# A two-layer decoder kernel: 28 passes in one turn of the loop in place of seven turns of four

## The chip, the cores and the metric

The kernel runs on one core of one Trainium2 chip. The metric is the device time of one execution in microseconds (us). Times of a kernel are medians over several executions; a profile is one further execution, recorded by the hardware profiler. The engines are TensorE (PE; its weight loads are listed as PEld), VectorE (DVE), ScalarE (ACT), GpSimd (POOL) and SyncE (SP), which here issues all the DMAs.

## What is computed

For each of 32 batches (256 tokens x 256 features) two decoder layers are computed, in float32:

```
x = x + latent_attention(layernorm(x))        # 16 heads, softmax over tokens
x = x + cross_attention(layernorm(x), ctx)    # 16 heads of 64, softmax over heads per token
x = x + routed_ffn(layernorm(x))              # the best 128 of 256 tokens go through the FFN
x = x + topk_attention(layernorm(x))          # the best 25 scores per row are kept
x = x + cross_attention(layernorm(x), ctx)    # masked by a length per batch
x = x + ternary_linear(layernorm(x))
```

## The kernel before, in words

The work on a batch is cut into four stages, each with a letter: **m** (latent attention), **h** (cross attention with the routed FFN), **t** (top-k attention), **c** (masked cross attention and the last linear layer). The stages form a pipeline over batches. In one *pass* m works on batch i+3, h on i+2, t on i+1 and c on i. A stage hands its rows to the next one through single buffers (`xin` from m to h, `xa` from h to t, `x4` from t to c), so a stage's next pass begins when the stage ahead of it has finished this one.

Each stage is written as a generator for each engine, and every `yield` in it ends a step. The order in which an engine's steps of the four stages are interleaved is a string of letters, one string for each engine (`ORDER["pe"]`, ...); `woven` takes one step of the named stage for each letter. Each engine executes its instructions in that order, and semaphore waits do the rest. The strings of `ORDER` hold four passes (`LAPS = 4`). The last letters of a string may name a stage whose four passes are already over; such a letter issues nothing.

`passes` emits one such stretch: a block with all five engines, then a second block in which SP clears all the semaphores. At the end of each block the engines meet in a barrier (lines 1295 and 1340 in the profile). The stretches are `start`, `first`, the loop, and `last`. The loop (line 1350) executes its one stretch of four passes seven times, jumps back after each time, and is called here seven *turns*. Since the semaphores are cleared, every count of a wait starts again in each turn. `past` emits a wait for the pass before, and emits none in a turn's first pass, where the barrier stands for it.

The instructions that stand around a turn's end and beginning, by line: L795 (PE) is the last matmul of stage h, and L919 (DVE) adds its result to `xa`, the last instruction of the turn on DVE. L712 (PE) projects `ctxA` for the next batch in stage h, and the first 16 of these matmul records are a turn's first on PE. L402, L406 and L419 (DVE) and L411 and L414 (POOL) are the layer norms; L429 (PE) transposes the normed rows; L442 and L450 (PE) are projections; L1020 (DVE) copies the values of stage t and is the first DVE instruction that needs a projection. SP's queue loads `ctxB` and the length (L1303), `xin` (L1310) and `ctxA` (L1313), and stores the result (L1317), in this order in each pass.

Of the kernel before, what the change touches and what calls it, by code (L numbers as in the profile page):

```python
# [133 lines left out]
        t5 m t h t h m t3 h t2 h c2 t h c t7 h2 t4 m t3 h2 t2 c t h t6 c t2 h t m t h c h t3 h t3 c t9 h t3 h m h t3 m t2 h t c t c t h t2 h  # L134
        c t4 h2 t2 m t2 c t3 h2 m t9 h c2 t2 h t h t h t6 c t2 h t7 h t2 m t h t3 m h t h t2 c3 t2 h t4 h2 t h t5 m t3 h2 t3 h t5 c h t2"""),
}
LAPS = 4

FILL = {"t": ["00020100", "02010111", "00020101", "02010011"],
        "h": ["20111000100", "00211000000", "00121000100", "01111100000"],  # L140
# [24 lines left out]
def program(nc, x_in, ctx_in, lens_in, w_in, out):  # L165
    es = ExitStack()
    with es:
# [196 lines left out]
        lap = {"n": 0}  # L364
        first, last = {}, {}
# [27 lines left out]
        def fill(letter, place, to):  # L393

            table = {"loop": FILL, "first": FILL_FIRST, "last": FILL_LAST}.get(lap["of"], {})
            if letter in table:
                for _ in range(int(table[letter][lap["n"] - first[letter]][place])):
                    nc.tensor.matmul(to, w["xwq"][:, 0, 0:P], w["xwq"][:, 1, 0:P], start=True, stop=True)

        def ln_dve(dve, k, x, ln):  # L400
# [279 lines left out]
        def tensor_h(pe):  # L680
# [34 lines left out]
            for s in range(QUADS + 3):  # L715
# [21 lines left out]
                if s >= 3:  # L737
                    q = s - 3
                    yield
                    pe.wait_ge(*at(g["hm_pt"], q + 1))  # L740
                    fill("h", q, bankH[1][:, D:D + P])
                    for uh in range(2):
                        for jo in range(2):
                            i = jo * 2 + uh
                            last = nc.tensor.matmul(bankH[1][jo * XD:(jo + 1) * XD, uh * P:(uh + 1) * P],
                                                    xv[:, 4 * q + i, :], xpt[q % 2][:, i, :], start=True, stop=True)
                    last.then_inc(g["hm_o"], 1)
# [11 lines left out]
            for d in range(ND):  # L759
                last = nc.tensor.matmul(bankH[0][:, 0:S], w["wrt"][:, d, :], lnH["xT"][:, d, :], start=(d == 0), stop=(d == ND - 1))  # L760
            last.then_inc(g["md_sps"], 1)
            fill("h", 8, bankH[1][:, 0:P])
            yield
            pe.wait_ge(*at(g["md_e"], 6))
            fill("h", 9, bankH[1][:, D:D + P])
            for d in range(ND):
                for t in range(NT):
# [577 lines left out]
        nb = out.shape[0]  # L1345
        loops = (nb - 3) // LAPS
        rest = nb - loops * LAPS
        passes("start", m=(0, 0, 0))
        passes("first", m=(1, 0, 1), h=(0, 0, 1), t=(0, 1, 1))
        with nc.Fori(0, (loops - 1) * LAPS + 1, LAPS) as i:  # L1350
            passes("loop", m=(i + 3, 0, LAPS - 1), h=(i + 2, 0, LAPS - 1), t=(i + 1, 0, LAPS - 1), c=(i, 0, LAPS - 1))
        spans = dict(h=(nb - rest + 2, 0, rest - 3), t=(nb - rest + 1, 0, rest - 2), c=(nb - rest, 0, rest - 1))
# [73 lines left out]
```

## Time and profile before

| what | value |
|---|---|
| time, median of 3 runs | 6089.8 us (6071.2 to 6093.05) |
| the profiled execution: span from first to last instruction | 6105.9 us |
| PE busy | 5431.5 us (89% of the span) |
| DVE busy | 4571.6 us (75%) |
| ACT busy | 3697.2 us (61%) |
| POOL busy | 2166.8 us (35%) |

The profile has no time of its own beside its span; the span is 16.1 us over the median of the runs. A busy share is an average over the whole span. What happens at a turn's end is to be read from the stretch around it.

### The profile page before, as it was taken

How to read it: one execution, taken by the hardware profiler on the slowest of the kernel's cores; microseconds unless marked ns; L12 is line 12 of the kernel's file. 1: busy time of each engine (PE TensorE's matmuls, PEld its weight loads, DVE VectorE, ACT ScalarE, POOL GpSimd, SP SyncE). 2: the span in 40 equal slices, each digit the busy share in tenths (PEclk: the TensorE clock that was granted, in tenths of full speed). 3: DMA queues.
4: the chain of work that ended last, by engine and by line, in shares of the span. 5: the costliest groups of instructions: out<-in, count | busy, mean ns of one | idle time of the engine just before them, and what ended most of it. 6: DMA issues, size and time to landing. Idle time of an engine off the chain costs nothing. (4 is left out here: it accounts for less than half of the span.)

```text
span 6105.9 us, 112143 instructions
## 1 busy us (share of the span) xinstructions
PE 5431.5 (89%) x39450; PEld 3840.7 (63%) x39450; DVE 4571.6 (75%) x16189; ACT 3697.2 (61%) x9249; POOL 2166.8 (35%) x3076
## 2 busy tenths in 40 slices
PE   7899998889898899889988898988898889898987
PEld 4666666666666666666666666666666666666654
DVE  2477887777886777887776887777887777887784
ACT  3465666656666655666665666656666556666642
POOL 0233443333343333433333433333433333433331
PEclk7799999999998999999999999999999999998976
DMA  2000000000000000000000000000000000000000
GB/s 87 4 5 6 8 8 6 7 6 6 8 6 8 6 6 6 6 10 8 5 6 8 6 8 7 6 7 6 8 8 6 7 6 6 8 6 6 5 5 6
DMA packets 29372, 53.32 MB, mean 9 GB/s; under 512 B 8145, under 2 KB 9810, under 8 KB 27986
## 3 DMA queue, kind: packets, MB, share of 16 engines
q1 hardware_dynamic: 28770, 45.73, 2.4%
q8 instruction: 324, 5.31, 0.4%
q14 instruction: 278, 2.28, 0.1%
HBM read 37.33 MB, written 8.39 MB: 7 GB/s over the span
## 5 line engine op out<-in xcount | busy, mean ns | idle before, releaser
L1044 DVE MATCH_REPLACE8 wk<-m,wk 128x256 f32<-128x256 f32 x2048 | 820.8, 408 | 0.0
L1065 POOL TENSOR_SCALAR mx<-m 128x2 f32<-128x2 f32 x512 | 120.9, 236 | 1933.8 <-DVE wk L1044 1931.5
L479 DVE TENSOR_REDUCE m_nm<-bankM 128x2 f32<-128x512 f32 x1024 | 650.9, 680 | 158.9 <-PE bankM L469 156.7
L1040 DVE MAX8 m<-wk 128x8 f32<-128x256 f32 x2048 | 758.2, 411 | 0.0
L1074 POOL TENSOR_TENSOR t_pr<-t_pr,sc 128x512 f32<-128x512 f32 x512 | 651.9, 1273 | 40.2
L810 ACT ACTIVATE xk_area<-bankH,xb 64x256 f32<-64x256 f32 x1024 | 479.7, 468 | 297.1 <-PE bankH L712 278.5
L1072 POOL TENSOR_TENSOR t_pr<-wk,sc 128x512 f32<-128x512 f32 x512 | 658.4, 1286 | 2.1 <-PE bankT L570 0.9
L1001 ACT ACTIVATE t_pr<-t_pr,t_nm 128x256 f32<-128x256 f32 x1024 | 464.6, 507 | 212.4 <-POOL t_pr L1074 212.0
L528 PE MATMUL bankM<-m_q,m_kT 32*128 32x512 f32 x2048 | 567.6, 634 | 0.0
L469 PE MATMUL bankM<-m_kT,m_q 32*128 32x256 f32 x4096 | 532.5, 398 | 9.8 <-DVE m_nm L479 8.7
L570 PE MATMUL bankT<-ident,t_pr 128*128 128x128 f32 x2048 | 346.1, 294 | 146.3 <-ACT t_pr L1001 144.0
L469 PEld LDWEIGHTS bankM<-m_kT,m_q 32*128 32x128 f32 x4096 | 379.4, 193 | 82.3 <-issue 25.6
L579 ACT ACTIVATE t_pt<-bankT 128x512 f32<-128x512 f32 x512 | 308.2, 602 | 193.1 <-PE bankT L570 189.4
L570 PEld LDWEIGHTS bankT<-ident,t_pr 128*128 128x128 f32 x2048 | 239.8, 147 | 285.3 <-ACT t_pr L1001 234.0
L542 ACT ACTIVATE m_pT<-bankM,keymask 128x512 f32<-128x512 f32 x512 | 338.0, 692 | 130.2 <-PE bankM L528 127.3
L1044 DVE MATCH_REPLACE8 wk<-m,sc 128x256 f32<-128x256 f32 x1024 | 410.6, 408 | 0.0
L1044 DVE MATCH_REPLACE8 wk<-m_last,wk 128x256 f32<-128x256 f32 x1024 | 410.5, 408 | 0.0
L1040 DVE MAX8 m<-sc 128x8 f32<-128x256 f32 x1024 | 379.2, 411 | 35.4 <-ACT sc L991 33.9
L555 PE MATMUL bankM<-m_pT,m_va 128*32 128x256 f32 x4096 | 368.6, 441 | 18.0 <-ACT m_ot L562 14.5
L991 ACT ACTIVATE sc<-bankT 128x512 f32<-128x512 f32 x512 | 306.3, 602 | 121.2 <-PE bankT L469 118.1
L1040 DVE MAX8 m_last<-wk 128x8 f32<-128x256 f32 x1024 | 378.9, 412 | 0.0
L875 DVE TENSOR_REDUCE xnm<-bankH 128x4 f32<-128x512 f32 x256 | 175.0, 684 | 253.0 <-PE bankH L735 253.0
(223 smaller groups left out, 11963.2 us busy)
## 6 DMA issues: line engine op xcount, KB each, us to landing
xin<-x_in SPq DMA_DIRECT2D x32, 256.0 KB, 2.6
ctxA<-ctx_in SPq DMA_DIRECT2D x32, 256.0 KB, 2.6
ctxB<-ctx_in SPq DMA_DIRECT2D x32, 256.0 KB, 2.7
out<-x SPq DMA_DIRECT2D x32, 256.0 KB, 2.0
w<-w_w SPq DMA_DIRECT2D x2, 1024.0 KB
xwq<-w_xwq SPq DMA_DIRECT2D x1, 1024.0 KB
xwk<-w_xwk SPq DMA_DIRECT2D x1, 1024.0 KB
xwv<-w_xwv SPq DMA_DIRECT2D x1, 1024.0 KB
```

What stands on the lines that cost most here:

```text
L469: last = nc.tensor.matmul(bank[x][:, j * S:(j + 1) * S], b["q2"][r:r + 32, e, j, t * P:(t + 1) * P], b["kT"][r:r + 32, e, :], start=not ma ...
L479: nc.vector.tensor_reduce(b["nm"][:, i % 2, 2 * (i // 2) + x, :], banks[u % 4][:].rearrange("p (j s) -> p j s", j=2), AX.X, ALU.max, negat ...
L528: nc.tensor.matmul(bank[x][:], b["kT"][r:r + 32, e, c * P:(c + 1) * P], b["q2"][r:r + 32, e].rearrange("p j s -> p (j s)"), start=False, s ...
L542: nc.scalar.activation(b["pT"][c][:, x, :], bank[(0, 1, 3)[(2 * i + x) % 3]][:], ACT.Exp, bias=0.0 if bias is None else bias[:, c:c + 1]). ...
L555: last = nc.tensor.matmul(bank[r:r + 32, S * (m % 2):S * (m % 2 + 1)], b["va"][:, c, 4 * m + 2 * x + j, :], b["pT"][c][:, x, S * j:S * (j ...
L570: last = nc.tensor.transpose(bank[:, (2 * c + j) * P:(2 * c + j + 1) * P], b["pr"][:, u % 2, j, c * P:(c + 1) * P], w["ident"][:])
L810: nc.scalar.activation(dst[0:XD, :, 8 * h:8 * h + 8].rearrange("p (j a) u -> p j a u", a=2), bankH[1 - TURNS.index("vqk"[which] + str(quad ...
L1001: nc.scalar.activation(b["pr"][:, u % 2, t, :], sp_[:, u % 2, t, :], ACT.Exp, bias=b["nm"][:, u, t:t + 1], scale=-1.0 / BIG).then_inc(g["s ...
L1040: link.inc(nc.vector.max(top, src[:, t, :]))
L1044: m = nc.vector.match_replace(out=wk[:, k, t, :], in_to_replace=take, in_values=src[:, t, :], imm_value=-BIG)
L1072: nc.gpsimd.tensor_tensor(taken[:, u % 2], wk[:, u % 2], sc[:, u % 3], ALU.subtract).then_inc(g["sp_tk"], 1)
L1074: nc.gpsimd.tensor_tensor(sp_[:, u % 2], taken[:, u % 2], sc[:, u % 3], ALU.mult).then_inc(g["sp_mul"], 1)
```

## The change

`LAPS` becomes 28, so the loop makes one turn. Each engine's string is cut to whole passes (the letters that issue nothing go) and said seven times over. The filler matmuls' table is read modulo its four passes. Counts of semaphores run on over 28 passes, and `past` now emits its waits in all passes but the first. The stretches `start`, `first` and `last` stay as they are.

```diff
-LAPS = 4
+PLANNED = 4
+LAPS = 28
+
+
+def whole(order):
+
+    seen, kept = collections.Counter(), []
+    for letter in order:
+        seen[letter] += 1
+        if seen[letter] <= order.count(letter) // PLANNED * PLANNED:
+            kept.append(letter)
+    return "".join(kept)
+
+
+ORDER = {engine: whole(order) * (LAPS // PLANNED) for engine, order in ORDER.items()}
...
-                for _ in range(int(table[letter][lap["n"] - first[letter]][place])):
+                for _ in range(int(table[letter][(lap["n"] - first[letter]) % len(table[letter])][place])):
```

On PE, before, a turn ends with these rows, with the semaphores that each waits for in brackets; `hm_`, `md_` and `ln1_` belong to stage h, `spa_` and `ln3_` to t, `crs_` and `ln4_` to c, `mla_` to m.

```order
L450 MATMUL bankT<-swo,lnT_xT 128x256 [waits spa_onT]
L450 MATMUL bankT<-swo,lnT_xT 128x256 x3
L795 MATMUL bankH<-xv 128x256 [waits md_yff]
L795 MATMUL bankH<-xv 128x256
L1295 UNCONDITIONAL_BRANCH
L1350 REGISTER_ALU [waits barrier_Pool_Activation_PE_DVE_SP_release]
L1350 COMPARE_AND_BRANCH
```

The jump leads back to the first rows of the same turn, where PE waits for nothing but the transfer of `ctxB`. After the change (line numbers are 15 higher) the same place in the program reads as follows.

```order
L465 MATMUL bankT<-swo,lnT_xT 128x256 [waits spa_onT]
L465 MATMUL bankT<-swo,lnT_xT 128x256 x3
L810 MATMUL bankH<-xv 128x256 [waits md_yff]
L810 MATMUL bankH<-xv 128x256
L727 MATMUL bankH<-ctxA,xwv 128x256 [waits ctxA_in,md_yff]
L727 MATMUL bankH<-ctxA,xwv 128x256 x3
L727 MATMUL bankH<-ctxA,xwv 128x256 [waits md_x3]
L727 MATMUL bankH<-ctxA,xwv 128x256 x3
L457 MATMUL bankM<-ctxB,cwk 128x256 [waits ctxB_in,mla_pv]
L457 MATMUL bankM<-ctxB,cwk 128x256 x3
```

No row has changed its place among the matmuls: the two branch rows and the barrier between them are gone, and the waits for `ctxA_in`, `md_yff`, `md_x3` and `mla_pv` have come in. On DVE, before, the turn ends like this.

```order
L663 TENSOR_TENSOR x<-bankT,x3b 128x512 [waits spa_y,stored,sp_xb]
L919 SCALAR_TENSOR_TENSOR xa<-bankH,gate,xa 128x256 [waits md_e,md_xh,md_u]
L919 SCALAR_TENSOR_TENSOR xa<-bankH,gate,xa 128x256
L1295 UNCONDITIONAL_BRANCH
L1350 REGISTER_ALU [waits barrier_Pool_Activation_PE_DVE_SP_release]
L1350 COMPARE_AND_BRANCH
```

After the change DVE goes straight on to the layer norms of the next pass.

```order
L678 TENSOR_TENSOR x<-bankT,x3b 128x512 [waits spa_y,stored,sp_xb]
L934 SCALAR_TENSOR_TENSOR xa<-bankH,gate,xa 128x256 [waits md_e,md_xh,md_u]
L934 SCALAR_TENSOR_TENSOR xa<-bankH,gate,xa 128x256
L417 BN_STATS lnF_st<-x 128x6 [waits ln0_xn,spa_x]
L417 BN_STATS lnF_st<-x 128x6
L421 BN_AGGR lnF_mv<-lnF_st 128x2 [waits ln4_stat]
L421 BN_AGGR lnF_mv<-lnF_st 128x2
L417 BN_STATS lnH_st<-xin 128x6 [waits md_x3,mla_x]
```

Here too only the branches have gone; the new waits (`spa_x`, `ln0_xn`, `md_x3`, `mla_x`) are for results of DVE itself.

## Rows read from the trace of the kernel before

**Rows 1.** The page: span, and busy time of PE with its share.

```profile
span 6105.9 us, 112143 instructions
...
PE 5431.5 (89%) x39450; PEld 3840.7 (63%) x39450; DVE 4571.6 (75%) x16189; ACT 3697.2 (61%) x9249; POOL 2166.8 (35%) x3076
```

**Rows 2.** Windows, one per turn: length, each engine's busy time, granted clock, DMA.

```profile
396.58:1127.28 730.70, 660.84 (x4922) 470.53 (x4922) 570.91 (x2020) 461.42 (x1156) 271.21 (x384) 0.95 0.02 7
1127.28:1861.10 733.82, 659.04 (x4922) 470.26 (x4922) 570.95 (x2020) 461.30 (x1156) 271.21 (x384) 0.96 0.02 7
1861.10:2598.30 737.20, 663.41 (x4922) 473.21 (x4922) 571.17 (x2020) 461.32 (x1156) 271.22 (x384) 0.95 0.02 7
...
4799.96:5533.42 733.46, 659.27 (x4922) 470.40 (x4922) 570.96 (x2020) 461.27 (x1156) 271.22 (x384) 0.96 0.02 7
```

**Rows 3.** Timeline of DVE, first to second turn: start, duration, instruction, [idle before <- releaser].

```profile
1124.95 0.88 DVE L919 SCALAR_TENSOR_TENSOR xa<-bankH,gate,xa 128x256 f32<-128x256 f32 x2
1130.40 0.75 DVE L402 BATCH_NORM_STATS2 lnF_st<-x 128x6 f32<-128x256 f32 x2 [4.57 <-issue]
...
1149.62 0.69 DVE L1020 TENSOR_TENSOR t_va<-bankT,sbv 128x512 f32<-128x512 f32 x1 [9.38 <-PE bankT L450]
```

**Rows 4.** Timeline of PE in the same stretch.

```profile
1123.88 1.03 PE L795 MATMUL bankH<-xv 128*128 128x256 f32 x4
1130.54 6.08 PE L712 MATMUL bankH<-ctxA,xwv 128*128 128x256 f32 x16 [5.63 <-issue]
...
1139.91 0.60 PE L429 MATMUL bankT<-ident,lnT_xn 128*128 128x128 f32 x4
```

**Rows 5.** The loop's line 1350 on PE's sequencer: count, duration in ns min/median/max.

```profile
L1350 PEldq COMPARE_BRANCH  x7: 79/3650/4000, 1126.8 to 5533.4; - x7
```

**Rows 6.** The barrier's line 1340: who waited for it (us in total, times).

```profile
  PE bankH L712: 39.2, 9
  DVE lnF_st L402: 27.5, 7
```

**Rows 7.** Windows by granted clock (the 1.00 or 0.50), entering first and second turn.

```profile
396.40:403.40 7.00, 6.95 (x32) 6.14 (x33) 4.83 (x19) 3.30 (x7) 1.90 (x4) 1.00 0.12 39
...
1128.50:1135.30 6.80, 4.76 (x11) 3.87 (x12) 3.72 (x15) 0.92 (x2) 1.74 (x4) 0.50 0.14 38
```

**Rows 8.** Timeline of PE, entering the first turn.

```profile
393.49 1.13 PE L795 MATMUL bankH<-xv 128*128 128x256 f32 x4
396.45 3.69 PE L712 MATMUL bankH<-ctxA,xwv 128*128 128x256 f32 x16 [1.83 <-PEq L1340]
...
403.43 0.60 PE L429 MATMUL bankT<-ident,lnT_xn 128*128 128x128 f32 x4
```

**Rows 9.** Timeline of DVE, entering the first turn.

```profile
394.66 0.87 DVE L919 SCALAR_TENSOR_TENSOR xa<-bankH,gate,xa 128x256 f32<-128x256 f32 x2 [4.33 <-PE bankH L795]
396.39 0.75 DVE L402 BATCH_NORM_STATS2 lnF_st<-x 128x6 f32<-128x256 f32 x2 [0.86 <-PEq L1340]
...
401.66 0.74 DVE L419 TENSOR_SCALAR lnT_xn<-xa,lnT_mv,lnT_rs 128x256 f32<-128x256 f32 x2 [1.10 <-POOL lnT_rs L414]
...
413.14 0.69 DVE L1020 TENSOR_TENSOR t_va<-bankT,sbv 128x512 f32<-128x512 f32 x1 [5.93 <-PE bankT L450]
```

**Rows 10.** Timeline of SP's queue: the first turn's last store, the second's first load.

```profile
1051.83 0.35 SPq L1317 DMA_DIRECT2D out<-x  x1
1127.28 0.33 SPq L1303 DMA_DIRECT2D ctxB<-ctx_in  x1
```

**Rows 11.** Timeline of PE, the same projection in the first and second turn.

```profile
431.91 3.53 PE L712 MATMUL bankH<-lnH_xT,xwq 128*128 128x256 f32 x8 [0.33 <-ACT xq_area L810]
...
1168.39 1.99 PE L712 MATMUL bankH<-lnH_xT,xwq 128*128 128x256 f32 x8 [0.33 <-ACT xq_area L810]
```

**Rows 12.** DMA queues in one turn (3332 to 4066 us): packets, MB, share.

```profile
q8 instruction: 41, 0.67, 0.4%
```

**Rows 13.** List of waits: PE's commonest wait for its instructions (total, times, longest).

```profile
PEld bankM L555 <- issue: 189.2, 342, 1.5
```

More of the change, by code:

```diff
@@ L1 @@
+import collections
 import numpy as np
```

## The prediction

> **What bounds the kernel now.** I read the page first. PE is busy for 89% of the span [rows 1], and no single wait on the page is long enough to explain the rest, so the question is where a turn loses time and whether the places that the change touches are among them. Next came one window for each turn [rows 2]. Seven turns take 730.70 to 737.20 us each, 5136.8 us together, and every turn has the same work: PE's, DVE's and POOL's busy times differ by less than 1%. The first turn is the shortest. It is the only one that is entered by falling into the loop; the six others are entered by the jump back. That difference is an experiment that the old kernel makes on itself, and most of what follows is read from it.
>
> The third view is the timeline around the end of the first turn, engine by engine [rows 3, 4]. DVE ends its last addition at 1125.83 (1124.95 + 0.88) and does nothing until 1130.40, an idle time of 4.57 us. PE ends L795 at 1124.91 and begins L712 at 1130.54, 5.63 us idle. Neither waits for data. The rows of line 1350 say for what: the jump back takes PE's sequencer 3650 ns in the median [rows 5], while the barrier and the clearing lie ahead of it. The list of who waited behind the barrier shows that this is no single case: DVE lost 27.5 us there in 7 entries and PE 39.2 us in 9 [rows 6]. PE also pays after the pause. From 1128.5 to 1135.3 the granted clock is 0.50, that is 1.2 GHz, and the first 16 records of L712 take 6.08 us; on entering the first turn, after an idle time of only 1.83 us, the clock stays at 1.00 (2.4 GHz) and the same 16 take 3.69 us [rows 4, 7, 8].
>
> What waits for this is DVE. Its instruction L1020 needs a projection of PE, and DVE is idle for 9.38 us just before it [rows 3]. So PE sets the pace at a turn's start, and DVE's own earlier start would be worth nothing if PE's did not move.
>
> **The change, part by part.** *The jump.* Six jumps back go (the seventh turn's exit and the entries of the other stretches stay). From the start of L919 to the start of L1020 a join takes 1149.62 - 1124.95 = 24.67 us in the second turn [rows 3] and 413.14 - 394.66 = 18.48 us in the first [rows 9], a difference of 6.19 us. It is made of two terms on PE [rows 4, 8]: the pause, 5.63 - 1.83 = 3.80 us, and the slow clock, 6.08 - 3.69 = 2.39 us. Both go, since PE then follows L795 with L712 at once.
>
> The row of the jump is 3650 ns on PE. The Trainium skill (Advanced Engine Details and Errata, section Control Flow Timing) gives about 108 ns for a compare-and-branch. By that figure six jumps would be worth 0.65 us, and with the barriers below the sum would be some 12 us, by an estimate from that page; the trace's 3650 ns speaks against using it here.
>
> *The barriers and the clearing.* What the first turn's entry still has, 1.83 us of PE [rows 8], is the two barriers and the clearing between them. That goes as well, six times. Is something else then last? The normed rows that PE transposes at 403.43 were ready at 402.40 (401.66 + 0.74), 1.03 us earlier [rows 8, 9]. PE moves up by 1.83 and DVE by the 0.86 that it waited [rows 9], so 1.03 - 1.83 + 0.86 = 0.06 us of slack is left: PE is still last, just. I take the whole 1.83.
>
> *Sum for one join:* 3.80 + 2.39 + 1.83 = 8.02 us; six joins give 48.1 us.
>
> *New waits.* PE now waits for `md_x3` (DVE's L919) ahead of its second group of L712. It gets there half of 3.69 us after 1124.91, at 1126.8, and L919 ends at 1125.83: the wait is met 0.9 us earlier. Behind it stands all of PE, so if DVE were late, everything would be; the 0.9 us is the cover. Its other new waits are for things finished long before. DVE's new waits are for its own results; I cost them at nothing, since they stand ahead of the 9.38 us in which DVE is idle anyway. The `ctxB` load, issued at 1127.28 after the jump, will follow the store of 1051.83 in SP's queue [rows 10], some 70 us ahead of its use, and can't be late.
>
> *What a moved start is worth at the turn's end.* The first turn shows this too. Its `ctxB` was issued at 396.58, and L1020 came 16.56 us later; in the second turn it was 22.34 us (1149.62 - 1127.28), so the first turn was 5.78 us ahead at that point. At its end it was 733.82 - 730.70 = 3.12 us ahead [rows 2, 3, 9, 10]. So 2.66 us were given back on the way. More than half of it is one place: at 431.91 eight records of L712 take 3.53 us where the second turn's take 1.99 [rows 11], 1.54 us more, as they do at half clock. That is no wait that a later engine imposes. It is the clock falling at another place than in the other turns. The third turn, entered with a jump like the second, is 3.38 us longer than it [rows 2], so such losses come with either entry. I take the mean over the seven turns, (2.66 + 3.38) / 7 = 0.86 us, as the toll of a turn: 8.02 - 0.86 = 7.16, six times 43 us. The bounds are 8.02 (no toll) and 5.36 (the first turn's toll in each), so 48 and 32 us.
>
> *Fetching of straight-line code* is an unknown cost, since no run shows 28 passes without a jump. From below it is nothing: a turn before fetches its instructions too, 41 packets on one of the two instruction queues [rows 12], so no code was kept from one turn to the next. From above, PE's commonest wait for its instructions inside a turn is at most 1.5 us, 189.2 us in 342 places [rows 13], and stays as it is. I take nothing.
>
> The sum is made from joins of an execution of 6105.9 us, and the median of the runs is 6089.8, 0.26% less. The joins are in every run, so I take the 43 us off the median: 6047 us, 0.7% faster. A measurement of this kernel can tell about 0.5%, 30 us, from no change.
>
> **The rivals.**
> *Larger:* the removal of the slow stretch at each turn's start also spares one later in the turn, worth another 1.54 us or more a turn [rows 11]. Six times 9.6 us give 58 us, 6032 us. Against it: the one entry at full clock had more such stretches, not fewer.
> *Swallowed:* DVE or a chain through POOL becomes last at the join, and only DVE's pause of 4.57 us [rows 3] goes, less a toll of 0.86: six times 3.7, 22 us, 6068 us. For it: only 0.06 us of slack by my own count. Against it: DVE's 9.38 us of idle time ahead of L1020.
> *The pause isn't the jump's:* PE stalls for code once in so many instructions, and the straight line has that stall too. Then only 1.83 us a join goes, 11 us, 6079 us. Rows 13 speak against it: inside a turn the stalls are at most 1.5 us in PE's commonest group, while the join's is 5.63. The figure of the Trainium skill (Advanced Engine Details and Errata, Control Flow Timing) would lead to this case.
> *Slower:* the clock. With no pause at the turns' starts all six run like the third and worse, with half-clock stretches in the thin part of the turn around L712's projections of queries. One such stretch costs 1.54 us [rows 11], the worst turn's excess is 3.38 us [rows 2]. It decides from 8.02 us a turn on, more than five such stretches a turn; for 0.5% slower it would need 8.02 + 30 / 6 = 13.1 us a turn, some 6120 us in all. No turn shows a third of that.
>
> **How the numbers follow.** The forecast (32 to 48 us off) has 0.72, larger 0.09, swallowed 0.10, the pause that stays 0.05, slower 0.04. The forecast and the larger case are faster by over 0.5%, and of the swallowed case a fifth, which gives 0.83; the rest of the swallowed case and the pause that stays are within 0.5%, 0.13; slower 0.04. The time is that of the forecast, 6047 us. The range takes 48 and 32 us, then the runs' own spread (18.6 us under and 3.3 us over the median), and on the upper side the swallowed case: 6089.8 - 48 - 19 = 6023, widened to 6020 for the larger case, and 6068, rounded up to 6070.
>
> **What would show it right or wrong.** In the changed kernel's timeline there should be six places where L810 (was L795) is followed by L727 (was L712) with no idle time, where those 16 records take about 3.7 us at a granted clock of 1.00, and where L934 to L1035 (was L919 to L1020) takes about 16.7 us instead of 24.67. From the store that ends one group of four passes to the store that ends the next, 726 to 727 us should pass, against 734. A pause of several us on PE put down to issue, in the straight line, would show the third rival; an idle time of PE ahead of L444 (was L429) that DVE ends would show the second; more half-clock stretches than before would show the toll that I have put at 0.86. The prediction is wrong if the joins shorten by 8 us and the groups of four passes don't.

## The result, and the profile after

The changed kernel takes 6045.2 us, median of 6 runs (6030.4 to 6060.2); the kernel before takes 6092.1 us, median of 6 runs (6071.2 to 6107.1). The ratio is 0.9928, with a 95% interval of 0.9906 to 0.9949: faster by 0.7%, or 47 us. The forecast was 6047 us. The runs of the two kernels spread over 30 and 36 us, two thirds of the effect and more, though the slowest run of the changed kernel is still faster than the fastest of the one before. The runs of most kernels below fall into two groups some 25 us apart, and a median depends on how many of its runs lie in each. So what follows is read from the traces first and from the times second.

The page of the changed kernel, span and busy times (answers to [rows 1]):

```profile
span 6038.6 us, 111759 instructions
PE 5405.3 (90%) x39450; PEld 3826.1 (63%) x39450; DVE 4567.4 (76%) x16189; ACT 3697.0 (61%) x9249; POOL 2170.1 (36%) x3076
```

The span is 67.3 us shorter than that of before, but that is not all the change's. In the two profiles the code ahead of the loop, which is the same in both, ends at 372.03 and 394.66 us (22.6 us apart; the last section shows where), and what stands behind the loop is 8.9 us longer after (583.2 us against 574.3; in the second profile of the changed kernel, e1_control below, it is 574.4 again). So I compare the loops. The kernel after jumps no more, but its stretch is still seven groups of four passes, and I go on calling these turns. A turn is measured from the start of one group's addition to `xa` (L934, before L919) to the next.

Windows of the changed kernel, one per turn (bounds; length; busy time of PE, PEld, DVE, ACT and POOL with instructions; granted clock; DMA share; GB/s), answers to [rows 2]:

```profile
372.03:1095.26 723.23, 654.00 (x4923) 466.21 (x4924) 569.82 (x2021) 461.08 (x1156) 271.75 (x384) 0.96 0.03 7
1095.26:1820.23 724.97, 657.12 (x4923) 469.22 (x4922) 570.00 (x2020) 461.31 (x1156) 271.81 (x384) 0.96 0.02 7
1820.23:2545.98 725.75, 656.57 (x4923) 468.78 (x4922) 570.96 (x2021) 461.29 (x1156) 271.20 (x384) 0.96 0.02 7
...
3273.01:4003.65 730.64, 663.57 (x4923) 472.67 (x4922) 570.01 (x2021) 461.41 (x1156) 272.25 (x384) 0.95 0.02 7
...
4730.50:5455.43 724.93, 657.01 (x4922) 468.81 (x4920) 569.98 (x2020) 461.32 (x1156) 272.08 (x384) 0.96 0.02 7
```

The six turns behind the first last 5455.43 - 1095.26 = 4360.2 us together; before, the same six starts lie 4406.6 us apart (1124.95 to 5531.56). That is 46.4 us, 7.74 us a turn, in this profile. The rows also show that a turn's length varies by 6 us with the same instructions: PE is busy 663.57 us in the longest and 656.57 in the third, at granted clocks of 0.95 and 0.96.

At the join to the second turn, the timelines of DVE and of PE (start, length, engine, line, operation, count, idle time before and what ended it; answers to [rows 3, 4]):

```profile
1095.26 0.88 DVE L934 SCALAR_TENSOR_TENSOR xa<-bankH,gate,xa 128x256 f32<-128x256 f32 x2
1096.05 0.74 DVE L417 BATCH_NORM_STATS2 lnF_st<-x 128x6 f32<-128x256 f32 x2
...
1100.34 0.74 DVE L434 TENSOR_SCALAR lnT_xn<-xa,lnT_mv,lnT_rs 128x256 f32<-128x256 f32 x2 [1.11 <-POOL lnT_rs L429]
...
1111.67 0.69 DVE L1035 TENSOR_TENSOR t_va<-bankT,sbv 128x512 f32<-128x512 f32 x1 [5.70 <-PE bankT L465]
```

```profile
1094.19 1.03 PE L810 MATMUL bankH<-xv 128*128 128x256 f32 x4
1095.06 3.62 PE L727 MATMUL bankH<-ctxA,xwv 128*128 128x256 f32 x16
...
1101.96 0.60 PE L444 MATMUL bankT<-ident,lnT_xn 128*128 128x128 f32 x4
...
1129.45 1.01 PE L585 MATMUL bankT<-ident,t_pr 128*128 128x128 f32 x4 [1.45 <-ACT t_pr L1016]
1130.44 3.25 PE L727 MATMUL bankH<-lnH_xT,xwq 128*128 128x256 f32 x8
...
1855.42 1.99 PE L727 MATMUL bankH<-lnH_xT,xwq 128*128 128x256 f32 x8 [0.34 <-ACT xq_area L825]
```

PE goes from L810 to L727 with no idle time and the 16 records take 3.62 us; DVE's pause of 4.57 us is gone too. From L934 to L1035 it is 1111.67 - 1095.26 = 16.41 us, and within 0.01 us of that at all six joins, against 24.67 at the same join before. But 35 us behind the turn's start, eight records of L727 take 3.25 us, where the same eight take 1.99 in the next turn. The windows of the granted clock show both places (answers to [rows 7]):

```profile
1090.00:1097.00 7.00, 7.00 (x35) 5.64 (x33) 2.40 (x8) 1.00 (x3) 0.00 (x0) 1.00 0.00 0
...
1129.00:1133.00 4.00, 3.55 (x10) 2.72 (x11) 3.22 (x9) 2.92 (x6) 1.75 (x4) 0.58 0.00 0
```

The jump runs once, at the exit, and PE's commonest wait for instructions is as it was (answers to [rows 5, 13]): the instructions of line 1365, and the list of waits (in total, times, longest).

```profile
L1365 PEldq COMPARE_BRANCH  x1: 84/84/84, 5457.3 to 5457.3; - x1
```

```profile
PEld bankM L570 <- issue: 186.5, 342, 1.5
```

SP's queue now has the next pass's load right behind the store (answers to [rows 10]):

```profile
1022.03 0.34 SPq L1332 DMA_DIRECT2D out<-x  x1
1024.06 0.33 SPq L1318 DMA_DIRECT2D ctxB<-ctx_in  x1
```

### The profile page after: what moved, and what is told of

Same layout as the page of the kernel before. It is cut to its first block and busy times, and to the rows that moved or that the text cites. A ratio compares the mean times of both kernels' runs of the same rounds, so it can differ in the third digit from the quotient of the medians.

```text
span 6038.6 us, 111759 instructions
## 1 busy us (share of the span) xinstructions
PE 5405.3 (90%) x39450; PEld 3826.1 (63%) x39450; DVE 4567.4 (76%) x16189; ACT 3697.0 (61%) x9249; POOL 2170.1 (36%) x3076
## 5 line engine op out<-in xcount | busy, mean ns | idle before, releaser
L1059 DVE MATCH_REPLACE8 wk<-m,wk 128x256 f32<-128x256 f32 x2048 | 834.5, 421 | 0.0
L1055 DVE MAX8 m<-wk 128x8 f32<-128x256 f32 x2048 | 770.8, 423 | 0.0
```

Of the source, the lines that this page charges most:

```text
L1055: link.inc(nc.vector.max(top, src[:, t, :]))
L1059: m = nc.vector.match_replace(out=wk[:, k, t, :], in_to_replace=take, in_values=src[:, t, :], imm_value=-BIG)
```

## The experiments

A *join* below is the time from the addition to `xa` to the copy of `t_va` at the second turn's start, a *turn* the time from one such addition to the next.

| run | join, us | turn, us | time, median (range, runs) | ratio to before (95%) |
|---|---|---|---|---|
| before | 24.67 | 733.9 (one 737.2) | 6101.3 (6072.9 to 6129.6, 20) and 6092.3 (6069.5 to 6106.6, 23) | |
| e1_control | 16.42 | 727.04 | 6036.7 (6032.9 to 6062.3, 7) | 0.9915 (0.9886 to 0.9944) |
| e2_written_out | 18.43 | 727.04 | 6056.3 (6034.6 to 6064.7, 8) | 0.9927 (0.9898 to 0.9956) |
| e3_pe_pause | 24.55 | 733.87 | 6099.7 (6067.5 to 6103.1, 12) | 0.9987 (0.9966 to 1.0007) |
| e4_filled | 16.42 | 723.62 | 6032.8 (6024.0 to 6043.9, 6) | 0.9893 (0.9862 to 0.9924) |
| e5_pe_pause_half | 21.17 | 730.45 | 6079.5 (6049.0 to 6094.7, 12) | 0.9984 (0.9966 to 1.0001) |
| e6_dve_pause | 21.25 | 730.45 | 6056.5 (6047.6 to 6083.7, 10) | 0.9957 (0.9937 to 0.9977) |
| e7_one_stretch | 16.42 | 727.04 | 6040.5 (6023.0 to 6061.6, 6) | 0.9926 (0.9903 to 0.9949) |
| e8_one_filled | 16.42 | 723.62 | 6032.8 (6020.5 to 6043.0, 6) | 0.9909 (0.9888 to 0.9930) |

The first time of before stands beside e1 to e4, the second beside e5 to e8. The six turns behind the first repeat to 0.15 us within a run, but for the one of before and the last of e7_one_stretch (723.85 us).

**e1_control.** The changed kernel again.

> The changed kernel once more, as the measure for the three beside it. Both theories expect 6045 us within the spread of its runs (6030 to 6060), and 16.4 us from L934 to L1035 at each of the six joins.

All six turns behind the first take 727.04 us and all joins 16.42: 4362.2 us together, 44.4 less than before's six. The joins are as in the first profile of this kernel; the turns are steadier. The eight projections 35 us behind the start run slowly in all six of them (in the first profile in five of six):

```profile
1129.71 3.20 PE L727 MATMUL bankH<-lnH_xT,xwq 128*128 128x256 f32 x8
```

**e2_written_out.** The kernel before, with the seven turns written one behind the other by the program that emits them. Barriers and clears stay between them, the jump goes.

```diff
-        with nc.Fori(0, (loops - 1) * LAPS + 1, LAPS) as i:
+        for i in range(0, loops * LAPS, LAPS):
```

> The kernel before with its seven turns written out one behind the other: the same barriers and clears, no jump back. My theory: the jump is what makes a join long, through its pause and the slow clock after it. Then all six joins look like the first turn's entry of before: about 1.8 us of idle time on PE, granted clock 1.00, 18.5 us from L919 to L1020, and about 2.1 us more a join than the changed kernel: 6045 + 12 = 6057 us. The rival (the barriers, with the draining and refilling of the engines, cost the time): joins of 22 us or more, and 6080 us or more.

The timelines of PE and of DVE in e2_written_out, at the second turn's join (line numbers as before):

```profile
1111.56 1.03 PE L795 MATMUL bankH<-xv 128*128 128x256 f32 x4
1114.36 3.69 PE L712 MATMUL bankH<-ctxA,xwv 128*128 128x256 f32 x16 [1.77 <-PEq L1340]
```

```profile
1112.62 0.88 DVE L919 SCALAR_TENSOR_TENSOR xa<-bankH,gate,xa 128x256 f32<-128x256 f32 x2
1114.35 0.75 DVE L402 BATCH_NORM_STATS2 lnF_st<-x 128x6 f32<-128x256 f32 x2 [0.86 <-PEq L1340]
...
1131.05 0.69 DVE L1020 TENSOR_TENSOR t_va<-bankT,sbv 128x512 f32<-128x512 f32 x1 [5.51 <-PE bankT L450]
```

PE's idle time falls from 5.63 to 1.77 us and its 16 records take 3.69, at full clock. So 3.86 + 2.39 us of the join were the jump's. With the barriers left in, a join is 2.01 us longer than the control's, and yet the turns are as long: with the jump alone gone, a turn is already 733.87 - 727.04 = 6.83 us shorter than before's usual one. Windows of one turn and of a stretch 245.9 us behind its start, in e2_written_out and then in e1_control:

```profile
1839.61:2566.66 727.05, 656.48 (x4922) 468.57 (x4922) 571.04 (x2021) 461.74 (x1156) 271.61 (x384) 0.96 0.02 7
2085.50:2092.30 6.80, 6.70 (x60) 4.37 (x62) 3.97 (x14) 4.74 (x15) 0.00 (x0) 1.00 0.01 2
```

```profile
1821.56:2548.60 727.04, 658.00 (x4923) 469.84 (x4922) 570.94 (x2020) 461.84 (x1156) 271.65 (x384) 0.96 0.02 7
2067.50:2074.30 6.80, 6.80 (x44) 3.89 (x44) 3.57 (x13) 3.06 (x12) 0.00 (x0) 0.50 0.01 2
```

The control has 6.8 us at half clock in that place, e2_written_out none. Aligned instruction by instruction, the turn with barriers is 2.01 us late behind the join, 0.71 late after 170 us, 2.75 us *ahead* after 260, and level again to 0.2 us from about 410 us on, where it has its own half-clock stretches (in all they come to 61.4 us of the turn, the control's to 58.0). The barriers are paid for at the join and are worth nothing over a turn. The two kernels' times overlap (6034.6 to 6064.7 us and 6032.9 to 6062.3). So it is luck that the median came out at the 6057 us that were expected: that figure was made from 2.1 us more a join, and the turns don't show them.

**e3_pe_pause.** The changed kernel, with PE alone held at each join until ACT has made ten copies into `t_pt`. No jump, no barrier, and DVE runs on.

```diff
+HOLD = 10
...
+                if n == 0 and joins():
+                    pe.wait_ge(g["hm_pause"], HOLD * joins())
...
+                for r in range(HOLD):
...
+                    nc.scalar.activation(bufT["pt"][:, r % 2].rearrange("p c s -> p (c s)"), w["xwq"][:, r % 2, 0:512], ACT.Copy).then_inc(g["hm_pause"], 1)
```

> The changed kernel with PE alone held at the six joins, by ten copies on ACT, for about 5.6 us; no jump, no barrier, DVE and POOL run on. My theory: PE sets the join, and a pause of that length brings the half clock with it. Then PE's first 16 records of L712 (here at a new line) take about 6.1 us instead of 3.6, the join takes 16.4 + 5.6 + 2.4 = 24.4 us, and the time returns to about 6085 to 6093 us. The rival (DVE or POOL sets the join): the join grows by less than 3 us and the time stays under 6065 us. If the pause comes without the slow clock, the join takes about 22 us and the time is 6079 us.

PE's timeline at the third turn's start, and the window of that turn:

```profile
1830.75 1.03 PE L816 MATMUL bankH<-xv 128*128 128x256 f32 x4
1837.17 6.19 PE L733 MATMUL bankH<-ctxA,xwv 128*128 128x256 f32 x16 [5.40 <-ACT t_pt L826]
```

```profile
1831.81:2565.68 733.87, 659.26 (x4922) 470.42 (x4922) 570.90 (x2021) 466.60 (x1167) 271.22 (x384) 0.96 0.02 7
```

A pause of PE about as long as the jump's (5.40 us against 5.63) brings back the slow 16 records (6.19 us against 6.08), the join of before (24.55 us; 24.4 were expected), the turn of before and the time of before (7 us above the range expected). ACT, which makes the copies, waits for PE at this place in the changed kernel too (4.13 us), so it loses little by them. The pause of PE and the clock behind it are enough to explain what the change gives, without DVE, the barriers or the fetched code. How much of it is the one and how much the other it can't tell, since the pause brings both.

**e4_filled.** The changed kernel, with five filler matmuls ahead of the transposes of `t_pr` for which PE waits 1.45 us, in the first pass of each group of four only: the place ahead of the half-clock stretch at 1130 us. The two waits there change places, so that the fillers run ahead of the one for ACT.

```diff
-            pe.wait_ge(*at(g[n + "_ex"], 2 * (u + 1)))
             pe.wait_ge(*at(g["sp_sc"], min(H, 2 * (u // 2 + 1) + u % 2 + 1)))
+            if u == 0 and lap["of"] == "loop" and (lap["n"] - first["t"]) % PLANNED == 0:
+                for _ in range(5):
+                    nc.tensor.matmul(bank[:, 0:P], w["xwq"][:, 0, 0:P], w["xwq"][:, 1, 0:P], start=True, stop=True)
+            pe.wait_ge(*at(g[n + "_ex"], 2 * (u + 1)))
```

> The changed kernel with five filler matmuls in each turn, where PE waits 1.45 us for ACT some 33 us after L934, just ahead of the stretch at half clock that five of its six joins show. My theory of the toll: PE's idle time there lets the clock fall. Then the stretch at 0.50 about 34 us behind L934 is gone in all turns, and 1.3 us in five or six turns come back: 6045 - 8 = 6037 us, which the time alone can hardly tell; the trace decides. The rival: the clock falls by something else; the stretch stays where it is and the time is that of the changed kernel, or a little above.

PE's timeline 33 to 35 us behind the second turn's start in e4_filled, then the windows of the third turn and of this place:

```profile
1135.61 1.38 PE L584 MATMUL bankT<-xwq 128*128 128x128 f32 x10
1137.14 0.66 PE L588 MATMUL bankT<-ident,t_pr 128*128 128x128 f32 x4
1138.13 1.99 PE L730 MATMUL bankH<-lnH_xT,xwq 128*128 128x256 f32 x8 [0.33 <-ACT xq_area L828]
```

```profile
1826.57:2550.19 723.62, 655.53 (x4933) 469.00 (x4932) 570.86 (x2020) 461.81 (x1156) 271.61 (x384) 0.96 0.02 7
1136.00:1140.00 4.00, 3.52 (x21) 2.66 (x20) 3.90 (x11) 3.59 (x8) 1.15 (x3) 1.00 0.02 4
```

The five fillers (ten records in the trace) fill the wait, the eight projections take 1.99 us at full clock in place of 3.20, and each turn is 3.42 us shorter than the control's, where 1.3 were expected. Only 1.2 us of it are gained at this place. Aligned with the control's, the turn is 1.20 us ahead behind the projections, 2.83 after 170 us, 6.23 after 260, 3.62 after 410 and 3.41 at its end, as its other half-clock stretches lie elsewhere; their sum over the turn is the control's, 58.0 us. So that stretch was a part of the toll, and one that can be had back; the other 2.2 us came with stretches that moved, and why they moved is open. The median of the times is the lowest with that of e8_one_filled, but 4 us below the control lies inside the spread; for that difference the trace alone speaks.

**e5_pe_pause_half.** As e3_pe_pause, with five copies in place of ten.

```diff
-HOLD = 10
+HOLD = 5
```

> The held PE with five copies on ACT in place of ten: about 3.3 us of idle time on PE at each of the six joins. If a turn's length follows its join, the join takes 16.4 + 3.3 = 19.7 us at full clock (22 us if the slow clock comes with it), the turn 727.0 + 3.3 = 730.3 us, and the time is 20 us above the control. The rival: a late start is worn away inside the turn, as the 2.0 us of the written-out turns were; then the turn takes 727.0 us again, with the half-clock stretches at other places, and the time is the control's.

PE's timeline at the second turn's start, and the window of that turn:

```profile
1092.77 5.41 PE L733 MATMUL bankH<-ctxA,xwv 128*128 128x256 f32 x16 [2.80 <-ACT t_pt L826]
```

```profile
1090.01:1820.47 730.46, 658.43 (x4922) 469.77 (x4922) 570.96 (x2021) 464.02 (x1162) 271.24 (x384) 0.96 0.02 7
```

PE is idle for 2.80 us and its 16 records take 5.41, at a granted clock of 0.68, so part of them run at half clock, and the join (21.17 us) lies between the 19.7 and the 22 us that were expected for either clock. Half the pause of e3_pe_pause costs half its turn's loss (3.41 of 6.83 us), as expected where a late start is not worn away. The times spread too widely to show it: the median is 43 us above the control's, where the six turns make 20.

**e6_dve_pause.** The changed kernel, with DVE alone held at each join until POOL has made three additions into `t_pr`; PE runs on.

```diff
+            if joins():
+                dve.wait_ge(g["crs_pause"], 3 * joins())
...
+                for r in range(3):
...
+                    nc.gpsimd.tensor_tensor(bufT["pr"][:, r % 2], w["sbo"][:].unsqueeze(1).broadcast_to([P, NT, D]), w["sbv"][:].unsqueeze(1).broadcast_to([P, NT, D]), ALU.add).then_inc(g["crs_pause"], 1)
```

> The changed kernel with DVE alone held at the six joins by three additions on POOL, for about 4.1 us; PE runs on. My count gave DVE little slack at the join (its normed rows are ready 0.7 us before PE gets to them). So about 3.4 us of it shows: 19.8 us from L934 to L1035 (other line numbers here), PE idle ahead of its transposes (L429 of before) and waiting for DVE. The rival (DVE's idle time ahead of L1035 covers it): the join stays at 16.4 us. The turn takes 727.0 us if a late start is worn away, 730.4 if it is not.

DVE's and PE's timelines at the second turn's start, and the window of the turn:

```profile
1094.65 0.75 DVE L417 BATCH_NORM_STATS2 lnF_st<-x 128x6 f32<-128x256 f32 x2 [3.82 <-POOL t_pr L1208]
```

```profile
1089.76 3.62 PE L727 MATMUL bankH<-ctxA,xwv 128*128 128x256 f32 x16
...
1099.75 0.66 PE L444 MATMUL bankT<-ident,lnT_xn 128*128 128x128 f32 x4 [2.92 <-DVE lnT_xn L434]
1100.24 3.51 PE L727 MATMUL bankH<-ctxA,xwv 128*128 128x256 f32 x8
```

```profile
1089.96:1820.42 730.46, 658.33 (x4923) 469.69 (x4922) 571.05 (x2021) 461.30 (x1156) 274.94 (x387) 0.96 0.02 7
```

Of DVE's 3.82 us, 2.92 come back as a wait of PE, ahead of the transposes of the normed rows; behind that wait the next eight records run near half clock (3.51 us against 1.89 in the changed kernel). The join is 4.8 us longer, more than DVE's own pause and than the 3.4 expected. So DVE stands close behind PE at the join, as the rival of the swallowed gain had it. It decides nothing only because its pause went together with PE's. The turns and the span (6047.1 us) are those of e5_pe_pause_half, and the median is 23 us lower all the same, so a difference of medians of that size says nothing here.

**e7_one_stretch.** The stretches `first`, loop and `last` become one, so the two barriers left around the 28 passes go too. The strings of the three are put one behind the other.

```diff
+ORDER_ALL = {e: cut(e, ORDER_FIRST[e], PASSES["first"]) + whole(ORDER[e]) * (LAPS // PLANNED) + cut(e, ORDER_LAST[e], PASSES["last"])
+             for e in ORDER}
...
-        passes("first", m=(1, 0, 1), h=(0, 0, 1), t=(0, 1, 1))
...
+        passes("all", m=(1, 0, nb - 2), h=(0, 0, nb - 1), t=(0, 1, nb), c=(0, 2, nb + 1))
```

> All 34 passes after the start in one stretch: the barriers and clears ahead of and behind the 28 passes go too, the order on each engine stays. If a barrier's pause at a join is worth its 2.0 us, the two joins (18.5 and about 17.4 us) become shorter by 1 to 2 us each, 3 us in all; if it is worn away, nothing. Either way the time is the control's within its spread.

The windows of the first and second turn:

```profile
366.31:1090.99 724.68, 656.40 (x4923) 467.70 (x4922) 570.64 (x2020) 461.59 (x1156) 271.73 (x384) 0.96 0.02 7
1090.99:1818.09 727.10, 658.07 (x4923) 469.84 (x4922) 570.96 (x2021) 461.84 (x1156) 271.70 (x384) 0.96 0.02 7
```

The first join falls from 18.49 us in the control to 16.42, and the one behind the last turn from 17.39 to 15.08, as expected for barriers that go, if a little more; the time (6040.5 us, range 6023 to 6062) can't be told from the control's.

**e8_one_filled.** e7_one_stretch with the fillers of e4_filled.

> One stretch, and the five filler matmuls at each of the seven places ahead of the half-clock stretch. Expected from the filled kernel: turns of 723.6 us in place of 727.0, about 20 us in all against the control, so 6030 us or a little less, the best of all here. If the turn's length falls back to 727.0, the fillers' gain hung on the exact position of the half-clock stretches.

Its turns are those of e4_filled (723.62 us), as expected, and its median the same 6032.8 us. The fillers' version of either kind has the shortest turns that I found; its median lies 12 us under the changed kernel's first and 4 under the control's, both less than the runs spread.

## Why the prediction was right

*The jump* (3.80 us of pause and 2.39 of slow clock): right, in size and in cause. e2_written_out takes the jump alone away and finds 3.86 and 2.39; e3_pe_pause puts the pause alone back and finds before's turn. The Trainium skill (Runtime: NRT & Kernel Launch, section Instruction fetch mechanics) says that a taken branch to code outside the window held makes the engine fetch before it can go on, while straight code is streamed; this case's traces agree (3650 ns in the median for the jump back [rows 5], and no new wait in 28 passes of straight code). They show the fetching too: in the 6 us behind each of the six turn ends before, the two instruction queues move five to eight packets, and at the same six places of e2_written_out at most one. The 108 ns that the prediction quotes for a compare-and-branch (the Trainium skill, Advanced Engine Details and Errata, section Control Flow Timing) come near the exit only, 84 ns; for a jump taken the measured one decides.

*The barriers and the clearing* (1.83 us): right at the join (2.01 us between e2_written_out and the control), but the step that takes it through to the turn's end failed. A turn with barriers and one without both take 727.04 us, so six times 1.83 us of the sum were not there. The whole 6.83 us a turn came with the jump.

*DVE's slack* (0.06 us): too small. The normed rows end at 1100.34 + 0.74 = 1101.08 and PE's transposes begin at 1101.96, 0.9 us later; e6_dve_pause finds the same slack, 3.82 - 2.92 = 0.90 us. My count moved DVE up by the barrier's 0.86 us alone, but on entering the first turn DVE had also waited for the length `lenb`; in the joined passes that load is issued before the join (at 1024.44 us) and the wait is gone. PE is last, as I took it, so the error cost nothing.

*New waits and the load of* `ctxB`: right. PE has no idle time between L810 and L727, and the load follows its store by 2.0 us.

*The toll of a turn* (0.86 us): mis-sized. The control's joins are shorter by 24.67 - 16.42 = 8.25 us and its turns by 733.87 - 727.04 = 6.83, so the toll is 1.42 us. It lay where I had looked for it in the first turn [rows 11], at the projections 35 us behind the turn's start: aligned with four of before's six turns, the control is 8.1 to 8.3 us ahead behind the join, 6.9 to 7.1 behind these projections, and stays near 6.9 to the turn's end. e4_filled gets back these 1.2 us there, and 2.2 us more elsewhere. More half-clock stretches than before, the sign that I had named for it, didn't come: they sum to 58.0 us of a turn in the control and to 61.4 or 64.9 in the usual turns of before. What counts is where they fall.

*The sum*: 8.02 - 0.86 = 7.16 a turn, 43 us. Measured: 46.4 us in the first profile and 44.4 in the control's, against a profile of before in which one turn was 3.4 us longer than the rest; against its usual turn 6.83 a turn, 41 us. The group of four passes was to take 726 to 727 us and took 727.04. The sum came out close partly by luck. Its two errors are of opposite sign: the join gained 0.23 us more than I said and the turn gave 0.56 us more back. And the 0.97 us a turn that it had left of the barriers behind the toll (1.83 - 0.86) stand for nothing that was found, while the jump was worth 6.83 over a turn in place of the 6.19 of its two terms. That the median lies within 2 us of the forecast is luck as well, with runs that spread over 30 us.

*The rivals.* That the pause isn't the jump's is refuted by e2_written_out; that the clock makes it slower, by every turn of the control. The swallowed gain is refuted for this change (PE is last, the join 16.42 us), though e6_dve_pause shows how near it stood. The larger gain didn't come with the change: the slow stretch that it was to spare stands in all six turns of the control. With five filler matmuls a turn the six turns are 64.9 us shorter than before's, more than its 58 us, but that is another edit.

## What to carry to other kernels

When one turn of a loop is entered without a jump, compare it with the others before anything else: it prices the jump, and the clock behind it, from the old kernel's own trace. Here the difference of the joins said 6.19 us and that of the whole turns 3.6, and 6.83 were measured. Follow such a gain to the turn's end and not only to the join, since PE's clock may give it back or add to it elsewhere; here 2 us of barriers were worth nothing over 727 us, and five matmuls in a wait of 1.45 us were worth 3.4, of which 1.2 at their own place. An engine with much idle time can still be close behind: hold it for a few us, alone, and see who waits.

## What was not expected of the hardware

**A turn's length doesn't follow its join.** Joins of 16.42 and 18.43 us gave the same 727.04; 21.17 and 21.25 gave the same 730.45, though PE paused in the one and DVE in the other; 24.55 gave 733.87. The four lengths found, 723.62, 727.04, 730.45 and 733.87, lie 3.41 to 3.42 us apart. (The turns of the changed kernel's first profile, which aren't steady, don't keep to these steps.) Between the kernels that I aligned, what moves them is which stretches run at half clock, and not how many: 58.0 us of the turn do in the control and in e4_filled, 61.4 in e2_written_out, which is as long as the control. Why the lengths fall into equal steps is open.

**Half clock with PE busy, ahead of the loop.** Windows of the same stretch of unchanged code, and of the first 360 us, in the profile of the changed kernel and then in that of before:

```profile
140.00:155.00 15.00, 15.00 (x74) 9.08 (x73) 1.55 (x4) 7.53 (x27) 2.08 (x2) 0.50 0.00 0
155.00:170.00 15.00, 14.30 (x112) 9.79 (x112) 2.51 (x7) 10.40 (x40) 4.07 (x4) 0.94 0.01 2
0.00:360.00 360.00, 296.62 (x1800) 201.93 (x1801) 174.09 (x591) 175.34 (x459) 79.37 (x117) 0.83 0.11 39
```

```profile
140.00:155.00 15.00, 15.00 (x71) 9.72 (x72) 2.32 (x6) 7.76 (x31) 3.12 (x3) 0.50 0.00 0
155.00:170.00 15.00, 15.00 (x70) 9.37 (x66) 1.43 (x4) 5.88 (x20) 1.04 (x2) 0.50 0.00 1
0.00:360.00 360.00, 300.89 (x1655) 199.86 (x1656) 156.44 (x517) 165.44 (x437) 68.82 (x105) 0.75 0.11 39
```

PE is busy without a gap from 140 to 155 us and the granted clock is 0.50 all the same, for longer in the one execution than in the other. The ten profiles reach the first turn's addition anywhere between 362 and 395 us, and the later, the lower the granted clock over their first 360 us: at 361.7 us with 0.86 (e5 and e6), at 366.3 and 366.4 with 0.85 (e7 and e1), at 371.3 to 372.2 with 0.83 (e3, the changed kernel and e8), at 376.1 with 0.81 (e4), at 382.4 with 0.79 (e2) and at 394.7 with 0.75 (before). So the 22.6 us ahead of the loop in the first section go with the clock, and the code there is the same. I take this for a part of the spread of 25 to 30 us in the times of every kernel here; but most kernels have one profile alone, and no run held the clock still, so that is not shown, and what sets it stays open.
